# Splitting the VectorE part of each norm and reordering four engine queues in a two-layer graph network

## The reference

```python
def gat(h, adj, W, a):                       # layer 0, twice
    Wh = h @ W
    e = leaky_relu(Wh @ a[:F] + swap(Wh @ a[F:]), 0.2)
    return softmax(where(adj > 0, e, NEG), axis=1) @ Wh
h = norm0(x + gat(gat(x, adj, W1, a1), adj, W2, a2))
x = norm1(h + relu(h @ w_ff1 + b_ff1) @ w_ff2 + b_ff2)
q, k = x @ Wq + bq, x @ Wk + bk              # layer 1, 8 heads of 32
attn = softmax(q @ k.T / sqrt(32))
out = sum((attn * (adj == r)) @ (x @ Wv[r] + bv[r]) for r in range(4))
x = norm2(x + out @ Wo + bo)
return norm3(x + gelu(x @ W1 + b1) @ W2 + b2)
```

## Time and profile before

| | us |
|---|---|
| median of 3 runs | 3147.11 |
| lowest and highest | 3146.8, 3148.77 |
| the profiled execution | 3145.98 |
| its span, first to last instruction | 3144.2 |
| one full step of the loop, start to start of the same instruction | 47.30 |

### The profile page before, as it was taken

The page is one execution under the profiler, slowest core; times in us unless marked ns, Lnnn a source line. Parts: engine busy times, 40 slices in busy tenths (PEclk is TensorE's granted clock), DMA queues, the critical chain, the costliest instruction groups (busy, mean ns, idle before and its releaser), DMA issues.

```text
span 3144.2 us, 78504 instructions
## 1 busy us (share of the span) xinstructions
PE 3034.5 (97%) x26980; PEld 2739.5 (87%) x26980; DVE 2228.3 (71%) x4975; ACT 2434.3 (77%) x6218; POOL 1876.3 (60%) x1747
## 2 busy tenths in 40 slices
PE   5799999999999999999999999999999999999997
PEld 4788888888888888888888889889889889889885
DVE  4677777677777777777777777777777777777763
ACT  3578878878878878878778778788787787787774
POOL 3365665665665665665665665665666666666663
PEclk7899999999999999999999999999999999999998
DMA  3000100100100100100100100100100100100100
GB/s 143 25 22 24 33 27 23 33 27 23 33 27 23 33 27 23 33 27 23 33 27 23 33 27 23 33 27 23 33 27 23 33 27 23 33 27 23 33 12 14
DMA packets 101943, 93.54 MB, mean 30 GB/s; under 512 B 14736, under 2 KB 101008, under 8 KB 101776
## 3 DMA queue, kind: packets, MB, share of 16 engines
q1 hardware_dynamic: 101904, 93.00, 9.6%
HBM read 76.17 MB, written 16.78 MB: 30 GB/s over the span
## 4 chain that ended last, share of the span: by engine, by line
PE 90%; DVE 7%; ACT 1%; issue 1%; POOL 0%; DVEq 0%; DMA 0%; POOLq 0%; SPq 0%; ACTq 0%
PE ps_f L290 11%; PE ps_f L292 10%; PE ps_f L291 10%; PE ps_ao L487 7%; PE ps L477 6%; PE ps L290 5%; PE ps L291 5%; PE ps L292 5%; PE ps L467 4%; PE ps_ao L290 4%; PE ps_ao L532 4%; PE ps_g L291 3%; PE ps_g L290 3%; PE ps_g L292 3%; PE ps_ao L291 3%; PE ps_ao L292 3%
## 5 line engine op out<-in xcount | busy, mean ns | idle before, releaser
L1026 POOL TENSOR_TENSOR hid_lo<-hid_full,hid_hi 128x512 fp32r<-128x512 f32 x512 | 672.4, 1313 | 409.7 <-ACT hid_hi L648 390.6
L290 PE MATMUL ps_f<-down_w_hi,hid_hi 128*128 128x256 f32 x2048 | 592.9, 290 | 1.3 <-POOL hid_lo L1026 1.3
L1003 POOL TENSOR_TENSOR rstd<-vareps,neg_half 128x2 f32<-128x2 f32 x256 | 218.2, 852 | 610.7 <-DVE vareps L821 610.7
L291 PE MATMUL ps_f<-down_w_lo,hid_hi 128*128 128x256 f32 x2048 | 575.1, 281 | 0.0
L292 PE MATMUL ps_f<-down_w_hi,hid_lo 128*128 128x256 f32 x2048 | 574.8, 281 | 0.0
L665 ACT ACTIVATE prob<-ps,s_least 128x256 f32<-128x256 f32 x1024 | 469.4, 489 | 6.0 <-DVE s_least L869 5.2
L869 DVE TENSOR_REDUCE s_least<-ps 128x4 f32<-128x1024 f32 x256 | 309.4, 1209 | 140.4 <-PE ps L467 140.3
L290 PEld LDWEIGHTS ps_f<-down_w_hi,hid_hi 128*128 128x128 f32 x2048 | 385.6, 188 | 23.4 <-issue 19.9
L292 PEld LDWEIGHTS ps_f<-down_w_hi,hid_lo 128*128 128x128 f32 x2048 | 392.3, 192 | 0.0
L291 PEld LDWEIGHTS ps_f<-down_w_lo,hid_hi 128*128 128x128 f32 x2048 | 386.1, 189 | 0.0
L648 ACT ACTIVATE hid_hi<-hid_full 128x512 fp32r<-128x512 f32 x512 | 323.7, 632 | 16.3
(11 more groups left out here) (158 smaller groups left out, 9447.0 us busy)
## 6 DMA issues: line engine op xcount, KB each, us to landing
adj_in<-adj_keys SPq DMA_DIRECT2D x128, 256.0 KB, 2.9
xT_in<-x_features SPq DMA_DIRECT2D x64, 256.0 KB, 2.7
norm<-x_nodes SPq DMA_DIRECT2D x64, 256.0 KB, 2.7
out_nodes<-norm SPq DMA_DIRECT2D x64, 256.0 KB, 2.1
row_vectors<-all_row_vectors SPq DMA_DIRECT2D x1, 1536.0 KB, 10.4
raw_up<-L_w_ff SPq DMA_DIRECT2D x1, 1024.0 KB, 9.5
raw_down<-L_w_ff SPq DMA_DIRECT2D x1, 1024.0 KB, 11.7
raw_v<-L_Wv SPq DMA_DIRECT2D x4, 256.0 KB, 8.9
```

What stands on the lines that cost most here:

```text
L290: nc.tensor.matmul(ps_out, left[0], right[0], start=first, stop=False)
L291: nc.tensor.matmul(ps_out, left[0], right[1], start=False, stop=False)
L1026: pool.tensor_tensor(hid[1][:, 2 * m:2 * m + 2, :], hid_full[:, 2 * m:2 * m + 2, :], value(hid[0][:, 2 * m:2 * m + 2, :]), ALU.subtract).t ...
```

## The change

`dve_norm` ends behind the two `bn_stats`; the rest of it is a new function, `dve_spread`. Each body's queue gets a new order. Nothing else is changed: the same instructions with the same operands and waits.

In TensorE's body the up products 1 to 3 of layer 0 and the second scores move from the head of a step to the end of the step before, behind both pairs of turns; `pe_down(a, 0, 0, 1)` moves ahead of `pe_turn(d, 2)`; the last down product of layer 1 moves ahead of the products for e, and `pe_gat_wh1(e, 0)` behind the weighted sums. In VectorE's body `dve_gat_wh12(c, 1)` moves ahead of `dve_mask(b, 0)`, `dve_mask(b, 1)` and `dve_norm(c, 0)` ahead of `dve_fence(e)`, and the new `dve_spread` calls stand apart from their norms at two places: for norm 2 behind the `dve_gat_wh` of the next step, for norm 1 behind `dve_rec(b, 1, 1)`. In GpSimd's body `pool_affine` of norm 2 moves from the end of a step into the next one, behind `pool_gat_in`.

```diff
--- before.py
+++ after.py
@@ -537,21 +537,16 @@
 
             a, b, c, d, e = t + 1, t, t + 2, t - 1, t + 3
             if ff0:
-                pe_up(pe, a, 0, 1)
-                pe_up(pe, a, 0, 2)
-                pe_up(pe, a, 0, 3)
-            if att1:
-                pe_scores(pe, b, 1)
-            if ff0:
                 pe_down(pe, a, 0, 0, 0)
             if gat:
                 pe_gat_mix(pe, c, 0)
                 if isinstance(t, int) and t == -1:
                     pe_up_setup(pe, 1)
+            if ff0:
+                pe_down(pe, a, 0, 0, 1)
             if ff1:
                 pe_turn(pe, d, 2)
             if ff0:
-                pe_down(pe, a, 0, 0, 1)
                 pe_down(pe, a, 0, 1, 0)
                 pe_down(pe, a, 0, 1, 1)
             if gat:
@@ -591,27 +586,32 @@
                 pe_turn(pe, c, 0)
             if ff1:
                 pe_down(pe, d, 1, 1, 0)
+                pe_down(pe, d, 1, 1, 1)
             if nxt:
                 pe_gat_rows(pe, e)
                 pe_gat_cols(pe, e)
-            if ff1:
-                pe_down(pe, d, 1, 1, 1)
+            if att1:
+                pe_av_all(pe, b, 1)
+                pe_av_one(pe, b, 1)
+                pe_av_more(pe, b, 1)
             if nxt:
                 pe_gat_wh1(pe, e, 0)
                 if isinstance(t, int) and t == -3:
                     pe_up_setup(pe, 0)
-            if att1:
-                pe_av_all(pe, b, 1)
-                pe_av_one(pe, b, 1)
-                pe_av_more(pe, b, 1)
+            if gat:
+                pe_up(pe, c, 0, 0)
+            if att1:
+                pe_wo(pe, b)
             if ff0:
                 pe_prob_turn(pe, a, 0, 0)
-            if gat:
-                pe_up(pe, c, 0, 0)
-            if att1:
-                pe_wo(pe, b)
-            if ff0:
                 pe_prob_turn(pe, a, 0, 1)
+            if gat:
+                pe_up(pe, c, 0, 1)
+                pe_up(pe, c, 0, 2)
+            if ff0:
+                pe_scores(pe, a, 1)
+            if gat:
+                pe_up(pe, c, 0, 3)
 
 
         def act_gat_pre(act, g, l):
@@ -688,11 +688,14 @@
         def act_body(act, t, nxt, gat, ff0, att1, ff1):
 
             a, b, c, d, e = t + 1, t, t + 2, t - 1, t + 3
+            if ff0:
+                act_hidden(act, a, 0, 0)
             if gat:
                 act_gat_exp(act, c, 0)
                 if isinstance(t, int) and t == -2:
                     act_qkv_setup(act)
             if att1:
+                act_prob_turned(act, b, 0, 0)
                 act_prob_turned(act, b, 0, 1)
             if ff0:
                 act_hidden(act, a, 0, 1)
@@ -711,12 +714,13 @@
                 act_prob_turned(act, b, 1, 0)
             if ff0:
                 act_norm_end(act, a, 1)
-                act_turned(act, a, 1)
             if gat:
                 act_gat_exp(act, c, 1)
                 if isinstance(t, int) and t == -2:
                     act_up_setup(act, 1)
                     act_down_setup(act, 1)
+            if ff0:
+                act_turned(act, a, 1)
             if ff1:
                 act_hidden(act, d, 1, 0)
             if att1:
@@ -734,17 +738,14 @@
             if ff0:
                 act_prob(act, a, 0, 0)
                 act_prob(act, a, 0, 1)
+            if att1:
+                act_ao(act, b, 1)
+            if nxt:
+                act_gat_pre(act, e, 0)
+            if ff1:
+                act_norm_end(act, d, 3)
             if nxt:
                 act_gat_wh(act, e, 0)
-                act_gat_pre(act, e, 0)
-            if att1:
-                act_ao(act, b, 1)
-            if ff0:
-                act_prob_turned(act, a, 0, 0)
-            if ff1:
-                act_norm_end(act, d, 3)
-            if gat:
-                act_hidden(act, c, 0, 0)
 
 
         def dve_gat_in(dve, g):
@@ -812,6 +813,9 @@
             dve.wait_ge(*ysum[n](g, 1))
             for i in range(C):
                 dve.bn_stats(stats[n][:, i, :], y[:, i, :]).then_inc(stat_set[n].sem, 1)
+
+        def dve_spread(dve, g, n):
+
             dve.wait_ge(*stat_set[n](g, 2))
             dve.sem_inc(gate_v.sem, 1)
             for i in range(C):
@@ -918,55 +922,63 @@
             a, b, c, d, e = t + 1, t, t + 2, t - 1, t + 3
             if gat:
                 dve_gat_wh(dve, c, 0)
+            if ff1:
+                dve_spread(dve, d, 2)
+            if gat:
                 dve_gat_split(dve, c, 0)
                 if isinstance(t, int) and t == -2:
                     dve_qkv_setup(dve)
                     dve_rows_setup(dve)
             if att1:
+                dve_rec(dve, b, 0, 0)
                 dve_least(dve, b, 1, 0)
-                dve_rec(dve, b, 0, 0)
+                dve_rec(dve, b, 0, 1)
+            if gat:
+                dve_gat_wh12(dve, c, 1)
+            if att1:
                 dve_mask(dve, b, 0)
-                dve_rec(dve, b, 0, 1)
                 dve_least(dve, b, 1, 1)
+            if ff1:
+                dve_turned(dve, d, 2)
+            if att1:
+                dve_reach(dve, b)
                 dve_rec(dve, b, 1, 0)
-            if gat:
-                dve_gat_wh12(dve, c, 1)
-            if ff1:
-                dve_turned(dve, d, 2)
-            if att1:
-                dve_reach(dve, b)
             if ff0:
                 dve_norm(dve, a, 1)
             if att1:
                 dve_rec(dve, b, 1, 1)
+            if ff0:
+                dve_spread(dve, a, 1)
+            if att1:
                 dve_v(dve, b, 0)
             if gat:
                 dve_gat_score(dve, c, 1)
             if att1:
                 dve_v(dve, b, 1)
                 dve_flag(dve, b)
+            if gat:
+                dve_gat_wh(dve, c, 1)
+            if att1:
                 dve_v_more(dve, b)
                 dve_mask_more(dve, b, 0)
             if ff0:
                 dve_turned(dve, a, 1)
             if gat:
-                dve_gat_wh(dve, c, 1)
                 dve_gat_split(dve, c, 1)
                 if isinstance(t, int) and t == -1:
                     dve_up_setup(dve, 1)
                     dve_bias_setup(dve, 1)
             if att1:
                 dve_ao(dve, b, 0)
+                dve_mask(dve, b, 1)
+            if gat:
+                dve_norm(dve, c, 0)
+                dve_spread(dve, c, 0)
             if nxt:
                 dve_fence(dve, e)
-            if gat:
-                dve_norm(dve, c, 0)
-            if nxt:
                 dve_gat_in(dve, e)
                 if isinstance(t, int) and t == -3:
                     dve_up_setup(dve, 0)
-            if att1:
-                dve_mask(dve, b, 1)
             if ff0:
                 dve_least(dve, a, 0, 0)
             if gat:
@@ -974,18 +986,19 @@
                 if isinstance(t, int) and t == -2:
                     dve_qkv_bias_setup(dve)
                     dve_qkv_lo_setup(dve)
+            if att1:
+                dve_mask_more(dve, b, 1)
             if ff0:
                 dve_least(dve, a, 0, 1)
+            if ff1:
+                dve_norm(dve, d, 3)
+                dve_spread(dve, d, 3)
             if nxt:
                 dve_gat_wh12(dve, e, 0)
             if att1:
-                dve_mask_more(dve, b, 1)
-            if ff1:
-                dve_norm(dve, d, 3)
+                dve_ao(dve, b, 1)
             if ff0:
                 dve_adj_top(dve, a)
-            if att1:
-                dve_ao(dve, b, 1)
             if nxt:
                 dve_gat_score(dve, e, 0)
                 if isinstance(t, int) and t == -3:
@@ -1040,8 +1053,6 @@
 
             a, b, c, d, e = t + 1, t, t + 2, t - 1, t + 3
             if ff1:
-                pool_hidden(pool, d, 1, 0)
-                pool_hidden(pool, d, 1, 1)
                 pool_hidden(pool, d, 1, 2)
                 pool_hidden(pool, d, 1, 3)
             if gat:
@@ -1050,6 +1061,8 @@
                 pool_gat_in(pool, e)
                 if isinstance(t, int) and t == -3:
                     pool_down_setup(pool, 0)
+            if ff1:
+                pool_affine(pool, d, 2)
             if gat:
                 pool_affine(pool, c, 0)
                 if isinstance(t, int) and t == -2:
@@ -1071,10 +1084,11 @@
                 pool_rstd(pool, c, 1)
             if ff0:
                 pool_rec_wide(pool, a, 1)
-            if att1:
-                pool_affine(pool, b, 2)
             if ff1:
                 pool_affine(pool, d, 3)
+            if att1:
+                pool_hidden(pool, b, 1, 0)
+                pool_hidden(pool, b, 1, 1)
 
 
         def rows(w):
```

More of the change, by code:

```diff
@@ L602, in pe_body @@
                     pe_up_setup(pe, 0)
-            if att1:
-                pe_av_all(pe, b, 1)
-                pe_av_one(pe, b, 1)
-                pe_av_more(pe, b, 1)
-            if ff0:
-                pe_prob_turn(pe, a, 0, 0)
             if gat:
@@ L613, in pe_body @@
             if ff0:
+                pe_prob_turn(pe, a, 0, 0)
```

(11 more changed lines are left out.)

## The result

| | before | after |
|---|---|---|
| median, us | 3146.95 (4 runs) | 3166.16 (4 runs) |
| the profiled execution, us | 3145.98 | 3167.61 |
| its span, us | 3144.2 | 3165.8 |
| a full period, mean of 60, us | 47.30 | 47.68 |

The ratio is 1.0065, with a 95% interval of 1.0051 to 1.0079: slower, by 19 us. Before, each took 47.30 us. After, three lengths alternate: 47.33 (22 of 60), 47.82 and 47.92.

A forecast was written before the change was run, and what follows sets the result against it. TensorE's own work (busy 97% of the span) plus its waits bounds the kernel. A full period gains +0.9 - 0.09 - 0.09 = +0.72 us, times 61 is 43.9 on 3145.98: 3189.9, median 3191 us; range 3135 to 3206.

The forecast's parts named there:

- The masks: VectorE's first masks, behind the mix: a GpSimd affine half gets between them, V products 0.9 us late; bounds 0 and 1.2.
- The first rival: First masks lose nothing, the affine coming behind the second: -11 us, 3136 to 3147, most likely 3139; chance 0.27.
- The reciprocal: `dve_rec(b,1,1)` on VectorE's chain to the V copy moves into the pause behind the statistics: gain 0.09 us a period.
- The up product's wait: TensorE's second up product no longer waits for `ysum[2]`, both turn pairs standing ahead: gain 0.09 us, bounds 0 and 0.1.
- TensorE's total work is then the same: All TensorE instructions: none added or removed, as many changes between products and turns, so no change in its work.
- the moved block: First up product of layer 0, now behind weighted sums instead of turns: 0 to plus 0.1 us a period, taken as 0.
- the 3 us allowed: Start and end of the program, reordered too, their waits not in the sum: 3 us allowed either way.
- Nothing for the other moves: Fence, store, `sp_edges1` and GpSimd's moved affines: off the chain or covered, about 2 us spare for the edges; no price.

The follow-up runs named there:

- e5: The changed kernel with one wait more: GpSimd's `pool_affine` of norm 1 waits until both first masks are done; 3106.18 us, 0.9872 of before.
- e9: The kernel before with the first masks behind the small copy, and `pool_affine` of norm 1 waiting for both masks; 3145.60 us, 1.0002 of before.
- e2: The changed kernel with `pool_affine` of norm 1 over 8 of 256 columns for all graphs but the first; 3105.91 us, 0.9883 of before.
- e1: The changed kernel with the first masks again ahead of the small copy that waits for the mix; 3163.45 us, 1.0064 of before.
- e10: e5 with the last transposition of `pe_turn(a, 1)` issued twice; 3114.81 us, 0.9907 of before.
- e8: The kernel before with the last transposition of `pe_turn(a, 1)` issued twice; 3150.90 us, 1.0015 of before.
- e3: The kernel before with one part of the change alone, the first masks behind `dve_gat_wh12(c, 1)`; 3215.68 us, 1.0225 of before.
- e7: The kernel before with norm 1 split, the V copy ahead of its second half, `pe_turn(a, 1)` behind `pe_up(d, 1, 0)`; 3109.44 us, 0.9886 of before.
- e6: e5 plus the V copy ahead of `dve_spread(a, 1)` and `pe_turn(a, 1)` behind `pe_up(d, 1, 0)`; 3082.25 us, 0.9799 of before.

## Why the prediction was right and wrong, step by step

The direction and the mechanism were right, the size was not: 44 us forecast, 19 measured.

- *The masks.* Right in each step that the trace shows: small copy 0.20 us behind the mix, `rec_wide` just ahead of the first mask, the first affine half between the masks, pair 3.5 us (3.52). The norm's sum was forecast 0.9 us late and is 0.89 late (1.29 less 0.40). e5 and e9 keep the affine out of the masks by one wait and change nothing else, and the loss goes.
- *The first rival* needed the mask ahead of `rec_wide`. It was 0.20 us behind, so the chance hung on about as little as I had said. Whether a copy issued during a mask would have taken the turn stays open: in no run was one. The rival's size was wrong: without the meeting the change is not 11 us faster but 40 (e5). Of the 0.63 us a period, 0.45 is in "everything else", by the same step that failed in the forecast.
- *The reciprocal*, forecast 0.09: the second V product starts 2.75 us behind the norm's sum (1550.16 - 1547.41) and 2.85 before. *The up product's wait*, forecast 0.09: 1.80 less 1.67, 0.13. Both about right. In the one period shown the waits add 0.89 - 0.10 - 0.13 = 0.66 us; forecast 0.72. The mean over the periods is 0.98 - 0.24 - 0.13 = 0.61.
- **The step that failed** is the first of the parts: "TensorE's total work is then the same", with the moved block bounded at 0 and plus 0.1 us and taken as 0. The instructions are the same, but "everything else" in the table fell by 0.23 us a period. Over 60 periods that is 14 of the 25 us between forecast and result. The moved block itself was inside its bound (1.50 us instead of 1.46); what moved the sum are the others. The blocks behind the weighted sums take 0.18 less, since six of them run at 1.36 instead of 1.41 in 22 of 60 periods, the down blocks of layer 0 0.21 less, the up products of layer 0 0.18 more. The prediction took 1.36 for a block behind its like from one pair of rows, and had no row of the six blocks that run at 1.41 before. The bound should have been taken on all product blocks, not on one, and below zero as well.
- The rest: the waits were taken 0.11 us a period too large, 7 us. The profiled execution is 1.4 us above the median of its kernel, where I had counted 1.1 below: 2.6 us. And filling and emptying of the pipeline. The first output product came 2.9 us sooner, the last three periods took 2.6 us longer, what follows them 0.7 shorter: together some 1 us less, inside the 3 us allowed.
- *Nothing for the other moves*: right as far as the waits of TensorE show; `sp_edges1`, the fence and the store caused none.

**What stays open** is what sets the pace. Not the order alone: e5 and e2 run the blocks behind the weighted sums at 1.36 in every period, and e1, with TensorE's order the same, in 15 of 60, the others at 1.41. Not VectorE's and GpSimd's meeting as such: e9 has none at the first masks and runs at 1.41. One transposition more switched the block right behind it in e10, but not in e8, and in neither run the blocks behind the weighted sums. So what stands just ahead of a chain of products has a part in it, and doesn't decide it alone. The granted clock was 1.00 in all these stretches. Other shifts, and the addresses of the operands, were not tried.

## What to carry to other kernels

Before a VectorE instruction with two SBUF inputs is moved, lay GpSimd's timeline beside its new place: two long instructions of each, side by side, cost a whole instruction of the other engine even though no semaphore joins them (the pair lost 1.2 us after the change, 1.7 in e3), and the waits of the profile name the delay only at whoever waits last. Where such a meeting can't be avoided by the place, a semaphore wait on the engine with time to spare is the cheap cure (one wait took 60 us off here, e5, 48 of them as waits of TensorE). Only a meeting on the bounding engine's path needs it. And splitting a chain of small instructions pays where something else on the same engine ends a wait of the bounding engine: moving the V copy ahead of them, with the turn of norm 1 behind an up product, gave 1.1% in the old order (e7), pace included, and 2.0% against before with the new order and the wait (e6).

## What the runs showed of the hardware

VectorE and GpSimd take turns by whole instructions at SBUF where VectorE's has two SBUF inputs, and the one that waited goes next, even ahead of an instruction that stands directly behind on the other's queue. After the change the second mask, directly behind the first on its queue, was overtaken by an affine half that had been issued while the first ran (it took 2.27 us, 1.30 in e5); in e3 both engines alternated over four instructions (mask pair 4.06 us, affine half 2.15). The Trainium skill (GPSIMD Engine Reference, Key points) says that the two engines share SBUF interfaces and that GpSimd contends with VectorE instructions that have two SBUF inputs; the traces agree (the 3.52 and 2.27 us above), and show the turns beside it. A one-input GpSimd copy that had started 0.20 us ahead of the first mask cost little: the pair took 2.42 us in e5, and 2.36 in e9, where the copy had ended.

In these traces a chain of 128x256 products runs at one of two paces at the full granted clock, 0.113 or 0.118 us for each (1.36 and 1.41 for twelve). Both occur within one period, before (1.36 for the second up product of layer 0, 1.41 behind the weighted sums) and after. The same block may keep one of them in all periods (1.41 before, 1.36 in e5) or alternate (after). In after, a period with the blocks behind the weighted sums at the slower pace is 0.5 to 0.6 us longer (47.82 and 47.92 against 47.33), more than the 0.38 us that the whole change costs a period.
